# Layer 0 attention: value products per 128 queries in light-heavy order, output projection turned, with integer weights in two passes

## The reference, cut to what matters

```python
mod = silu(c) @ wmod                       # six rows of 512: sa, ca, ga, ...
h = layernorm(x) * (1 + ca) + sa
# q: 32 heads of 128; k, v: 8 heads of 128, each shared by 4 query heads
q, k, v = dequant_matmul(h, qw_q, scales_q), dequant_matmul(h, qw_k, scales_k), dequant_matmul(h, qw_v, scales_v)
q, k = rope(q), rope(k)
scores = q @ k.T / sqrt(128)               # causal: keys after the query masked
attn = softmax(scores)
ctx = attn @ v                             # 1024 x 128 per head
x = x + ga * dequant_matmul(ctx, qw_o, scales_o)    # (32 * 128) -> 512

def dequant_matmul(x, qw, scales):         # qw: integers 0..15, one scale per 128 input rows and column
    return x @ ((qw - 8) * repeat(scales, 128, axis=0))
```

## Time and profile before

| | us |
|---|---|
| median of 3 timed runs | 1865.25 |
| lowest and highest | 1859.18, 1865.29 |
| the profiled execution | 1857.97 |
| its span, first to last instruction | 1856.2 |
| TensorE busy in it | 1716.5 |
| VectorE, ScalarE, GpSimd busy in it | 1162.7, 808.8, 886.9 |

### The profile page before, as it was taken

How to read it: one execution, slowest core, us unless ns; L and a number is a source line. 1 busy time by engine, 2 the same in 40 slices (tenths; PEclk the granted TensorE clock), 3 DMA queues, 4 the chain that set the end, 5 groups by cost and what they waited for, 6 DMA issues and landing times. The chain is left out here.

```text
span 1856.2 us, 24749 instructions
## 1 busy us (share of the span) xinstructions
PE 1716.5 (92%) x8775; PEld 1251.9 (67%) x8775; DVE 1162.7 (63%) x2506; ACT 808.8 (44%) x1780; POOL 886.9 (48%) x786
## 2 busy tenths in 40 slices
PE   5699999999999999999999599998859999999778
PEld 3477777777777777777777388876735555554557
DVE  6866666666666666666655833345787766774475
ACT  3445454555545454555554211100315666667221
POOL 1687697786877968769673400000352222211200
PEclk9899999999999999999999799998869999999989
DMA  5111101011010101010100321103100000000021
GB/s 189 34 35 29 35 18 46 18 46 31 22 46 18 46 18 35 24 34 18 35 12 1 117 68 52 31 1 122 59 0 1 1 1 1 1 1 1 29 44 46
DMA packets 75315, 63.36 MB, mean 34 GB/s; under 512 B 23470, under 2 KB 53358, under 8 KB 75194
## 3 DMA queue, kind: packets, MB, share of 16 engines
q1 hardware_dynamic: 75194, 61.79, 11.1%
HBM read 59.68 MB, written 2.10 MB: 33 GB/s over the span
## 5 line engine op out<-in xcount | busy, mean ns | idle before, releaser
L844 ACT ACTIVATE a_probs<-psum,a_neg_max 128x128 f32<-128x128 f32 (+7 forms) x256 | 190.2, 743 | 240.3 <-DVE a_neg_max L768 240.0
L768 DVE CUSTOM_DVE_ANT_0 psum<-psum,a_keys_allowed 128x128 f32<-128x128 f32 (+7 forms) x256 | 195.1, 762 | 110.4 <-PE psum L77 110.1
L698 PE MATMUL psum<-a_probsT,a_v 128*128 128x512 f32 (+3 forms) x768 | 258.4, 486 | 0.2 <-ACT a_probsT L855 0.2
L698 PEld LDWEIGHTS psum<-a_probsT,a_v 128*128 128x128 f32 x768 | 144.6, 190 | 117.3 <-issue 91.8
L1717 ACT ACTIVATE a_probsT<-psum 128x512 f32<-128x512 f32 (+3 forms) x384 | 174.3, 497 | 86.5 <-PE psum L1554 62.6
L780 DVE SCALAR_TENSOR_TENSOR x<-psum,a_row_inv,x 128x512 f32<-128x512 f32 x256 | 191.0, 748 | 16.9 <-PE psum L77 10.7
L785 DVE TENSOR_TENSOR a_ctxT_lo<-psum,a_ctxT_hi 128x512 fp32r<-128x512 f32 x64 | 44.3, 692 | 216.0 <-ACT a_ctxT_hi L861 216.0
L855 ACT COPY a_probsT<-psum 128x512 f32<-128x512 f32 (+3 forms) x384 | 170.9, 484 | 9.8 <-PE psum L685 9.8
L685 PE MATMUL psum<-ident,a_probs 128*128 128x128 f32 x1152 | 171.6, 273 | 0.4 <-ACT a_probsT L855 0.4
L685 PEld LDWEIGHTS psum<-ident,a_probs 128*128 128x128 f32 x1152 | 138.7, 140 | 32.6 <-DVE x L780 4.7
L558 POOL TENSOR_TENSOR a_turned_pool<-a_q_sum,a_sine 64x512 f32<-64x512 f32 x62 | 79.9, 1288 | 167.0 <-DVE a_q_sum L754 165.9
(11 more groups left out here) (303 smaller groups left out, 4107.2 us busy)
## 6 DMA issues: line engine op xcount, KB each, us to landing
a_raw_q<-in_L_attn_qw_q SPq DMA_DIRECT2D x32, 256.0 KB, 4.1
a_raw_o<-in_L_attn_qw_o SPq DMA_DIRECT2D x32, 256.0 KB, 2.6
a_raw_scale_o<-in_L_attn_scales_o SPq DMA_DIRECT2D x32, 256.0 KB, 3.8
mod1b_w<-in_L_wmod SPq DMA_DIRECT2D x4, 1024.0 KB, 11.6
mod0a_w<-in_L_wmod SPq DMA_DIRECT2D x3, 1024.0 KB, 10.5
mod0b_w<-in_L_wmod SPq DMA_DIRECT2D x3, 1024.0 KB, 6.3
f_raw<-in_L_ffn_down_w SPq DMA_DIRECT2D x10, 256.0 KB, 3.1
f_raw<-in_L_ffn_gate_w SPq DMA_DIRECT2D x10, 256.0 KB, 3.3
```

Of the source, the lines that this page charges most:

```text
L698: last = nc.tensor.matmul(bank(use)[:, first:HALF], v[:, g % 2, j, :], probsT[b][:, j, first:HALF], start=(j == 0), stop=(j == keys - 1))
L768: nc.vector.tensor_tensor_reduce(out=scores, in0=scores, in1=keys_allowed[:, S - (i + 1) * P:S], scale=-1.0, scalar=-MASKED, op0=ALU.add, ...
L844: nc.scalar.activation(probs[:, u % 3, 0:(i + 1) * P], score[u % 2][:, 0:(i + 1) * P], ACT.Exp, bias=neg_max[:, h % 2, i:i + 1], scale=-1. ...
```

## The change

- The units of a head come in the order of tiles 0, 4, 1, 5, 2, 6, 3, 7. Scores of tiles 4 to 7 (heavy) use banks 0 and 1, those of 0 to 3 (light) bank 2, and the ring has five banks, 3 to 7.
- Value products are made per unit of 128 queries, two steps after the unit's own: i + 1 products of 128 columns. The turned probabilities are kept for two units, ctx for two heads.
- ScalarE scales each row of probabilities by its reciprocal row sum before it is turned (`weigh`), with one reciprocal on VectorE for each unit. Transposes wait for that.
- The output projection is turned: a block of 128 output features x 512 queries, weights (integer less 8) stationary, ctx's low and high part moving, two passes of 512 columns, eight blocks per head, two in each odd step. VectorE scales a block by a column of scale times gate and adds it to sumT, which is turned and added to x after the last head: 32 transposes and eight additions.
- Output weights are one conversion on ScalarE; GpSimd's four operations a head and the scale loads are gone. All 32 scale rows come in one load, are multiplied by the gate on GpSimd, turned by TensorE, copied by ScalarE. GpSimd clears sumT before its first rotary embedding.
- The partial sums of q's half 1 for head h+1 are made in steps 0 to 3 of head h, those of half 0 for head h+2 in steps 4 to 7; head 0 makes both halves for head 1 in steps 0 to 3. Loads of q and output weights have one buffer each.

The core of the diff:

```diff
...
-    units = [(h, i) for h in HEADS for i in tiles]
+    ORDER = [i for pair in zip(range(TPH), range(TPH, NT)) for i in pair]
+    units = [(h, i) for h in HEADS for i in ORDER]
...
-    RING = 4
+    RING = 5
...
-    def q_partial(h, i):
-        return (("q", h + 1, i // TPH), i % TPH) if h < LAST_HEAD else None
-
-    def kv_partial(h, i):
-        g, w = h // REP0, h % REP0 * NT + i
+    def q_partials(h, p):
+        due = [(h + 1, 1)] if p < TPH else [(h + 2, 0)]
+        if h == 0 and p < TPH:
+            due = [(1, 0), (1, 1)]
+        return [(("q", n, b), p % TPH) for n, b in due if n <= LAST_HEAD]
+
+    def outputs_due(h, p):
+        return [(h - 1, p - 1), (h - 1, p)] if h > 0 and p % 2 else []
...
-        score = mem.bank_pair
-        bank = lambda use: mem.bank[4 + use_at[use] % RING]
+        score = lambda i: mem.bank_pair[0] if i >= TPH else mem.bank[2]
+        bank = lambda use: mem.bank[3 + use_at[use] % RING]
...
+        def make_wo(act, h):
+            act.wait_ge(o_in, 16 * (h + 1))
+            if h >= 2:
+                act.wait_ge(*filled.of(("o", h - 2, NT - 1)))
+            nc.scalar.activation(wo[:, h % 2, :], raw_o[:, :], ACT.Copy, bias=-ZERO_POINT).then_inc(wo_made.sem, 1)
...
+        wo, sumT = sb("wo", [P, 2, D], F32R), sb("sumT", [P, KT, S])
...
+            sp.dma_start(scale_rows_o, scales["o"]).then_inc(tables_in, 16)
+            load_q(sp, 1)
...
-            def make_o(h):
...
-            pool.wait_ge(rope_in, 48)
+            pool.wait_ge(tables_in, 64)
+            pool.tensor_tensor(scale_rows_o, scale_rows_o, mem.gate[0:NH0, 0, :], ALU.mult).then_inc(drawn.sem, 1)
+            pool.memset(sumT[:, :, :], 0.0).then_inc(drawn.sem, 1)
+            pool.wait_ge(*drawn.of("sum"))
             turn(("k", 0, 0))
             turn(("k", 0, 1))
             for h in HEADS:
-                if h > 0:
-                    turn(("q", h, 1))
-                make_o(h)
                 if h < LAST_HEAD:
                     turn(("q", h + 1, 0))
                 if h % REP0 in (1, 2) and h // REP0 < LAST_GROUP:
                     turn(("k", h // REP0 + 1, h % REP0 - 1))
+                if h < LAST_HEAD:
+                    turn(("q", h + 1, 1))
...
-                pe.wait_ge(*exped.of((h, i)))
+                pe.wait_ge(*weighed.of((h, i)))
...
-            def values(h, b):
-
-                g, use = h // REP0, ("pv", h, b)
+            def values(u):
+
+                h, i = units[u]
+                g, use = h // REP0, ("pv", h, i)
                 wait_bank(use)
-                if h % REP0 == 0:
-                    pe.wait_ge(*v_taken.of((g, b)))
-                pe.wait_ge(*turned_out.of((h, TPH * (b + 1) - 1, b)))
-                keys = TPH * (b + 1)
-                for j in range(keys):
-                    first = max(0, j - TPH * b) * P
-                    last = nc.tensor.matmul(bank(use)[:, first:HALF], v[:, g % 2, j, :], probsT[b][:, j, first:HALF],
-                                            start=(j == 0), stop=(j == keys - 1))
+                if h % REP0 == 0 and i % TPH == 0:
+                    pe.wait_ge(*v_taken.of((g, i // TPH)))
+                pe.wait_ge(*turned_out.of(pieces_of(h, i)[-1]))
+                for j in range(i + 1):
+                    last = nc.tensor.matmul(bank(use)[:, 0:P], v[:, g % 2, j, :], probsT[:, u % 2, j, :],
+                                            start=(j == 0), stop=(j == i))
                 last.then_inc(filled.sem, 1)
 
-            def output(h, t):
-                use = ("o", h, t)
-                if t % TPH == 0:
-                    pe.wait_ge(*ctx_lo.of((h, t // TPH)))
-                if t == 0:
-                    pe.wait_ge(*o_made.of((h, "lo")))
+            def output(h, n):
+
+                (b, j), use = divmod(n, KT), ("o", h, n)
+                if j == 0:
+                    pe.wait_ge(*ctx_lo.of((h, b * TPH + TPH - 1)))
+                if n == 0:
+                    pe.wait_ge(*wo_made.of(h))
                 wait_bank(use)
-                split_products(nc.tensor, bank(use)[:, :], [part[:, tile(t)] for part in ctxT],
-                               [part[:, h % 2, :] for part in wo], True, True).then_inc(filled.sem, 1)
+                w = wo[:, h % 2, tile(j)]
+                nc.tensor.matmul(bank(use)[:, :], w, ctxT[1][:, h % 2, half(b)], start=True, stop=False)
+                nc.tensor.matmul(bank(use)[:, :], w, ctxT[0][:, h % 2, half(b)], start=False, stop=True).then_inc(filled.sem, 1)
...
+            def turn_sum(t):
+
+                use = ("x", t)
+                pe.wait_ge(*added.of((LAST_HEAD, t // TPH * KT + KT - 1)))
+                wait_bank(use)
+                for j in kts:
+                    last = nc.tensor.transpose(bank(use)[:, tile(j)], sumT[:, j, tile(t)], mem.ident[:, :])
+                last.then_inc(filled.sem, 1)
...
             for u, (h, i) in enumerate(units):
+                p = u % NT
                 if u + 1 < len(units):
                     scores(u + 1)
-                if h > 0:
-                    output(h - 1, i)
-                if q_partial(h, i):
-                    partial(*q_partial(h, i))
-                if kv_partial(h, i):
-                    partial(*kv_partial(h, i))
-                if v_turn(h, i):
-                    turn_v(*v_turn(h, i))
-                if values_due(h, i):
-                    values(*values_due(h, i))
+                for due in q_partials(h, p) + kv_partials(h, p):
+                    partial(*due)
+                for due in outputs_due(h, p):
+                    output(*due)
+                if v_turn(h, p):
+                    turn_v(*v_turn(h, p))
+                if u > 1:
+                    values(u - 2)
                 if u > 0:
                     turn_probs(u - 1)
+            values(len(units) - 2)
             turn_probs(len(units) - 1)
-            for t in range(TPH):
-                output(LAST_HEAD, t)
-            values(LAST_HEAD, 1)
-            for t in range(TPH, NT):
-                output(LAST_HEAD, t)
+            for n in first_half:
+                output(LAST_HEAD, n)
+            values(len(units) - 1)
+            for t in first_half:
+                turn_sum(t)
+            for n in second_half:
+                output(LAST_HEAD, n)
+            for t in second_half:
+                turn_sum(t)
...
-            def invert(h):
-                dve.wait_ge(*exped.of((h, NT - 1)))
-                nc.vector.reciprocal(row_inv[:, h % 2, :], row_sum[:, h % 2, :]).then_inc(inverted.sem, 1)
-                dve.wait_ge(*inverted.of(h))
-
-            def add_output(h, t):
-                use = ("o", h, t)
+            def invert(u):
+                h, i = units[u]
+                dve.wait_ge(*exped.of((h, i)))
+                nc.vector.reciprocal(row_inv[:, h % 2, i:i + 1], row_sum[:, h % 2, i:i + 1]).then_inc(inverted.sem, 1)
+
+            def add_output(h, n):
+
+                (b, j), use = divmod(n, KT), ("o", h, n)
+                total = sumT[:, j, half(b)]
                 dve.wait_ge(*filled.of(use))
-                nc.vector.scalar_tensor_tensor(out=mem.x[:, t, :], in0=bank(use)[:, :], scalar=row_inv[:, h % 2, t:t + 1],
-                                               in1=mem.x[:, t, :], op0=ALU.mult, op1=ALU.add).then_inc(added.sem, 1)
-
-            def split_values(h, b):
-                dve.wait_ge(*ctx_hi.of((h, b)))
-                nc.vector.tensor_tensor(ctxT[1][:, half(b)], bank(("pv", h, b))[:, :],
-                                        ctxT[0][:, half(b)].bitcast(F32), ALU.subtract).then_inc(ctx_lo.sem, 1)
+                if h == 0 and n == 0:
+                    dve.wait_ge(*drawn.of("sum"))
+                    dve.wait_ge(*scales_made.of("o"))
+                if h > 0:
+                    dve.wait_ge(*added.of((h - 1, n)))
+                nc.vector.scalar_tensor_tensor(out=total, in0=bank(use)[:, :], scalar=scale_o[:, j, h:h + 1], in1=total,
+                                               op0=ALU.mult, op1=ALU.add).then_inc(added.sem, 1)
+
+            def finish(t):
+                dve.wait_ge(*filled.of(("x", t)))
+                nc.vector.tensor_tensor(mem.x[:, t, :], mem.x[:, t, :], bank(("x", t))[:, :], ALU.add
+                                        ).then_inc(finished.sem, 1)
+
+            def split_values(h, i):
+                dve.wait_ge(*ctx_hi.of((h, i)))
+                nc.vector.tensor_tensor(ctxT[1][:, h % 2, tile(i)], bank(("pv", h, i))[:, 0:P],
+                                        ctxT[0][:, h % 2, tile(i)].bitcast(F32), ALU.subtract).then_inc(ctx_lo.sem, 1)
...
             for u, (h, i) in enumerate(units):
+                p = u % NT
+                invert(u)
                 if u + 1 < len(units):
                     maximum(u + 1)
-                if h > 0:
-                    if i == 0:
-                        invert(h - 1)
-                    add_output(h - 1, i)
```

(87 more changed lines are left out.)

161 lines of the change are left out of this document (77 added, 84 removed).

## The result

The changed kernel takes 1843.74 us (median of 4 runs, 1841.56 to 1846.85), the kernel before 1865.03 (4 runs, 1859.18 to 1865.29): a ratio of 0.9895, 95% interval 0.987 to 0.9919. Forecast were 1828 us and a range of 1803 to 1853. The direction and the range held; of 37 us forecast 21 came. The gain is clear of the noise, and about 1%. In profiled executions it is 1857.97 before and 1842.59 after, 15.4 us where the sum had 34. The changed kernel was not timed again beside the experiments, so between it and them a difference of a few us in time says nothing; head periods from the profiles say more.

What follows compares the result with a forecast made beforehand. TensorE's column passes were taken to bound the kernel. Terms -59.4 + 4 + 6 + 6.5 + 1 + 3.5 + 4.3 = -34 us took the profiled 1857.97 to 1824, forecast as a median of 1828, range 1803 to 1853.

Steps and rivals of the forecast that it cites:

- Output passes: Output projection on TensorE: 24 passes per head become 16, 1.86 us less per head, 59.4 us over 32 heads.
- Narrow values: Value products on TensorE: 72 passes of 128 columns at 0.1095 us, plus 0.13 us per head, 4 us in all.
- ScalarE's weighing: Eight scaled SBUF copies per head on ScalarE, about 5.1 us, costing nothing because ScalarE stays under TensorE.
- Chains in a step: Middle heads: dependent work across engines fits each step and the bank ring never stalls, except one wait, +6 us.
- The split of tile 3: Unit 4's step: ctx split late for the first output block, 0.22 us per head, some 28 times, +6 us (0 to 12).
- the prediction's own test: Prediction is wrong if the head period is over 29 us or a value pass takes over 0.12 us.
- Head 0: First head: about 5 us stall on GpSimd's rope, 1 us of slower clock, lost slack: +6.5 us (2 to 10).
- Last heads and tail: End of the attention phase: +4.3 us for the last four heads and +3.5 us for the tail.
- last group: Heads 28 to 31: even steps shorten without partials, the chains do not: +4.3 us (1 to 8).
- Rival 1: No new stalls, chains meet TensorE with room and head 0 loses 2 us: about 1808 us, chance 22%.
- Rival 2: Heavy chains 0.5 us longer than reckoned, stalls of 1 us per head eat the gain: 1856 us, chance 12%.
- Rivals 3 and 4: Slower: ScalarE's chain sets the pace, about 1911 us, 5%; weight loads set the short passes, about 2010 us, 3%.

Runs made afterwards that it cites:

- e8: The changed kernel without the weighing of probability rows on ScalarE, so TensorE's turns wait for the exponential alone: 1843.84 us.
- e7: The changed kernel with first partials ahead of the exponential from head 1, head 0's q halves made in turn, scale turns ahead of v's: 1816.71 us.
- e5: The kernel before with only its value products made narrow, 72 passes of 128 columns a head instead of 24 wide: 1866.6 us.
- e1: The changed kernel with ScalarE taking step 4's first q partial ahead of the next exponential, heads 1 to 31: 1833.37 us.
- e4: The kernel before with two output passes instead of three, the low part of the output weights left out: 1814.96 us.
- e9: The kernel before with two output passes and each step's output block ahead of its score products, on TensorE and VectorE: 1845.47 us.

## Why the prediction was right or wrong

**What bounds the kernel: right, until the change.** TensorE's columns set the end; taking a quarter of ScalarE's work away changed nothing (e8). VectorE's share was not tested.

**Output passes, -59.4: right.** Their starts in the middle, two blocks:

```profile
707.95 0.39 PE L712 MATMUL psum<-a_ctxT_lo,a_wo 128*128 128x512 f32 x1
708.18 0.40 PE L713 MATMUL psum<-a_ctxT_hi,a_wo 128*128 128x512 f32 x1
708.41 0.39 PE L712 MATMUL psum<-a_ctxT_lo,a_wo 128*128 128x512 f32 x1
708.64 0.40 PE L713 MATMUL psum<-a_ctxT_hi,a_wo 128*128 128x512 f32 x1
708.88 1.72 PE L699 MATMUL psum<-a_probsT,a_v 128*128 128x128 f32 x14
710.44 0.60 PE L687 MATMUL psum<-ident,a_probs 128*128 128x128 f32 x4
```

0.23 us each, 512 in all. e7, which has neither stall, gives the account of a head: 29.95 - 1.86 (output passes) + 0.29 (e5) = 28.38, and 28.05 was measured. The remaining 0.33 is mostly small waits that the kernel before had and e7 has not. Its list of waits from 95.7 to 874.7 us has, near the end,

```profile
PEld psum L685 <- DVE x L780: 4.5, 26, 0.2
```

and by start times 0.16 us a head are lost at that second turned piece of tile 5 and 0.15 at the output block of step 7 and the pass behind it. The prediction took the 29.96 for pure columns and did not see them.

**Narrow values, +4: right in mechanism, 0.13 us per head forecast, 0.29 measured.** 14 passes from 708.88 to 710.44 are 0.1115 us each and not 0.1095; 32 x 0.16 is 5 us more than forecast. The Trainium skill's ratio in "TensorE: Matmul & The Clock Gate", section "Back-to-back issue gap" (81 ns at 128 columns against 131 at 512), would have made them about 0.27 us by the prediction's estimate. The traces here do not agree with it, neither in these 14 passes nor in e5's row of 20.

**ScalarE's weighing, 5.1 us per head forecast, "costs nothing": right on the path, sized too small.**

```profile
L889 ACT ACTIVATE a_probs<-a_probs,a_row_inv 128x1024 f32<-128x1024 f32 x26 | 30.5, 1172 | 0.0
L889 ACT ACTIVATE a_probs<-a_probs,a_row_inv 128x128 f32<-128x128 f32 x26 | 10.5, 404 | 0.0
```

Eight of them are 6.3 us: the price at 128 columns was taken from a copy out of PSUM, and out of SBUF it is 0.404 us. From 128 to 1024 columns the price rises by 0.110 us per 128, so some 0.29 us of each is fixed. The Trainium skill's "VectorE: DVE Perf Modes", section on the TRN2 errata, names a fixed cost of each SBUF-source instruction, which these rows agree with; the estimate by its figures, 5.3, was below the measured 6.3 too.

**Chains in a step: the failed step.** The split of tile 3 was forecast at 0.22 us per head and is 0.25, and none of the heavy units' value products stalls in the middle. But the sentence "each of those is taken within about 4.8 us of the start of its step. No stall" was checked against the wrong limit. The bank of step 4's first use is wanted by step 5's first use. Step 4 is 3.26 us long and three score passes come ahead in step 5: 699.08 + 0.78 = 699.86, or 4.04 us after step 4's start at 695.82. ScalarE is done with it at 700.20, 4.38 us after that start, because the first partial stands behind the exponential of tile 6, which waits 1.3 us for VectorE. That is well inside 4.8, and too late. The chain had been followed for its own consumer, not for the banks of what is queued behind it. Price: 0.49 us per head in heads 1 to 27, 13 us, that the prediction put at nothing; e1 gave 0.48 back in the period, and 10 us in the time. With it and the 0.16 of the values, the 28.4 that was forecast becomes 29.1, and the 0.33 of the kernel before brings it back to the measured 28.79. That the two misses went against each other is luck: the prediction's own test (wrong over 29) did not trip, yet its chains had failed.

**Head 0, +6.5: right place, 1.5 us too small.** Of the 12.95, 5.0 is moved work and 8.0 is lost. The stall is 4.08 us, as told, by GpSimd's rope. The passes behind it, as the earlier trace rows led to expect, are at the lower clock, but for longer, and so are the loop's first ones:

```profile
74.33:78.00 3.67, 3.67 (x13) 3.20 (x13) 1.57 (x6) 2.41 (x5) 0.00 (x0) 0.52 0.00 0
95.11:98.60 3.49, 3.49 (x15) 3.02 (x15) 1.77 (x5) 2.47 (x6) 3.27 (x4) 0.53 0.02 5
```

Granted clock 0.52 and 0.53, nearly the lower level of 1.2 GHz. 3.5 us at half pace is 1.7 us lost where the forecast had 1. At the loop's start the forecast had nothing: the kernel before had the full clock from there (1.00 from 72.14 to 76.00 us). Why it was back sooner there is not shown.

**Last heads and tail, +7.8 together: some 5 us too small.** The chains that just fit in the middle do not where the partials are gone. In heads 28 to 31 the gaps before TensorE's value products, output blocks and partials sum to 7.6 us (0.48, 0.48, 0.83, 1.19, 0.37, 0.97, 0.84, 1.54, 0.93) where "last group" had 4.3. Six of the nine are value products behind ScalarE's turned copies, the longest of them the first of these two; the third row is in the tail:

```profile
989.05 1.80 PE L699 MATMUL psum<-a_probsT,a_v 128*128 128x128 f32 x14 [1.38 <-ACT a_probsT L897]
...
992.05 0.80 PE L699 MATMUL psum<-a_probsT,a_v 128*128 128x128 f32 x5 [0.77 <-ACT a_probsT L897]
...
1003.46 1.97 PE L730 MATMUL psum<-ident,a_sumT 128*128 128x128 f32 x16 [2.13 <-DVE a_sumT L813]
```

From the start of head 28's loop to the products of the last but one unit e8 takes the same time (108.58 us, 108.55 in the changed kernel), so it is not the weighing. The tail, from those products at 992.05 to 1006.91, is 14.9 us where 13.5 were forecast; TensorE waits 2.1 of it for VectorE's last addition to sumT before it turns it. No run changed either, so their causes are read from waits alone.

**Rivals.** Rival 1 (no stalls, 1808) lies 9 us below e7, 1816.7, which takes the middle's stalls out and still has those of the last heads. Rival 2 (stalls of 1 us per head eat the gain) is in part what happened: 0.74 us per head, two thirds of it at another place. Rivals 3 and 4 did not come.

## What to carry to other kernels

In a ring of banks, write for every use when its bank is wanted again (the same place in the next step) beside when its reader is done, and follow the reader's whole queue: an instruction that waits for another engine holds all the full banks behind it, and ScalarE, idle for 46% of the span, stalls TensorE once in every head here. Taking such a bank ahead of the waiting instruction brought no new wait of TensorE here; e1 is one condition and 10 us. Before a rewrite of the order, try its one certain saving in the old order: e4's edit is three lines, and beat the whole rewrite by 1.6% (timed on different occasions), at the price of the low part of wo, which integer weights do not have to pay.

## What was not expected of the hardware

- Behind even a short wait the next pass is late too: 0.34 us from the start of the first 512-column pass to the next instead of 0.23, after starts that were 0.1 to 0.4 us late, each in 27 of 27 heads (L651 in step 5 and L712 in step 1 of the changed kernel, the output block of step 7 in the kernel before). The wait therefore costs 0.1 us more than itself. The first score pass behind a row of transposes has 0.31 without any wait, and in e9 the late blocks that follow transposes have 0.34 against 0.31 of the others: there the wait adds little.
- How long the loop's start stays at the lower clock differs between profiles of the same code: 0.76 granted from 76 to 80 us in the changed kernel, 0.55 in e1.
- A float32 pass of 128 columns costs 0.1115 us in long rows (e5, 20 in a row), 4% over a quarter of the 0.43 of a 512-column one, though each weight load beside it is printed with 0.19.
- A copy with a scale from SBUF to SBUF on ScalarE costs 0.404 us at 128 columns, 1.172 at 1024; the copy out of PSUM was 0.280 at 128.
